# Local attention of a four-layer kernel: the next input's transposes in front of the second tile's scores, and their copy in front of the queries' squares

## The chip, the cores and the metric

The kernel runs on one core of one Trainium2 chip. Its time is the device time of one execution in microseconds; the median of three runs counts. A core has five engines with an instruction stream each: TensorE (PE, with its weight loads shown apart as PEld), VectorE (DVE), ScalarE (ACT), GpSimd (POOL) and SyncE (SP, which issues the DMAs). They run side by side and meet only at semaphores. Each engine works through its own stream in the order in which it is written.

## The reference

Four layers follow each other on an input of 32 sequences x 256 tokens x 128 features. The change touches the second, which runs twice (two local-attention blocks, each with a gated MLP behind it). Cut to what matters:

```python
x = x + layernorm(L0_attn(layernorm(x)))
x = x + layernorm(L0_ffn(layernorm(x)))       # two blocks of the kind below
x = x + layernorm(L1_attn(layernorm(x)))
x = x + layernorm(L1_ffn(layernorm(x)))

def _layer(x, ...):                           # 8 heads of 64, window 64
    h = shift_token(x)                        # half of the features from the token before
    q, k, v = split(h @ wqkv)
    q = l2norm(q) * qs; k = l2norm(k) * ksc
    q, k = rotary_xpos(q, k)
    o = local_attention(q, k, v)              # softmax over the own and the preceding window
    x = x + o @ wo
    ...                                       # gated MLP
```

## The kernel before

The function `window_attention` is built twice, as `w0` and `w1` (the page calls both `w`). A sequence of 256 tokens is one unit of work, two tiles of 128 tokens. A software pipeline of four stages runs over the 32 sequences: in step s, `ahead` is sequence s (its input is transposed), `front` is s-1 (keys, values and queries are projected, squared and turned), `back` is s-2 (scores, softmax, first tile's output) and `done` is s-3 (second tile's output, output projection). So 35 steps a layer; steps 0 to 3 and the last three are written out, those between are a loop of two steps a turn. In 29 steps of each layer (3 to 31) all four sequences exist.

The order on each engine is written by hand in its `step` function. The parts around the change:

- **TensorE** (`step`, L1428): keys of front, transposes KT, yT0, first half of the values V0, transposes QT, transposes P1 of done, masks and scores of tile 0 (job S0), attended values Y1 of done, V1, queries Q (L1376), transposes yT1 of done, masks and scores of tile 1 (S1, L1351 and L1364), the two transposes zT of ahead's input (L1392), transposes P0, the output projection "out" of done (L1469), attended values Y0 of back (L1414).
- **ScalarE** (`step`, L1310): squares and copy of the keys, copies kT, qT, pT of P1, yT0, V0, the exponentials of tile 0 (eight, L1305), copies of V1 and yT1 (L1269), squares of the queries (L1278), the two copies of zT into `hT` (L1334 for the features that stay, L1335 for those that are shifted by a token), copy of the queries (rawQ, L1269), the exponentials of tile 1.
- **VectorE** (`step`, L1205): among other work the maxima of tile 1's scores (L1180), the bias made from them (L1186, a 128x8 product), the copy of P0 out of PSUM (L1238), the lengths of the queries, and after Y0 its division (L1195).
- **GpSimd** (`step`, L1087): the rotary products of the keys and of the queries (two instructions each, L1071) and the powers of their lengths (L1084).

PSUM results go through rings of banks. The ring `short` has two banks and, in this order, six jobs a step: yT0, V0, V1, yT1, zT, out. Before TensorE writes a job (`wait_free`, L123) it waits until the job that had the same bank, two jobs earlier, has been copied out ("drained"). So V1 and zT share a bank, as do yT1 and out. "out" waits besides until zT has been copied (L1465), and so do the next sequence's keys (L1373). `hT` has one buffer: V1 and Q read it, then the copies of zT overwrite it.

Of the kernel before, what the change touches and what calls it, by code (L numbers as in the profile page):

```python
# [17 lines left out]
TILES = T // P  # L18
# [956 lines left out]
def window_attention(nc, n_seq, x, z, w, c, layer, shift, entry, following, leaving_stage):  # L975
# [14 lines left out]
    with ExitStack() as ctx:  # L990
# [49 lines left out]
        z_copy, copied = entry.z_copy, entry.copied  # L1040
# [13 lines left out]
        with nc.Block() as block:  # L1054
# [205 lines left out]
            @block.scalar  # L1260
            def _(act):
                act.wait_ge(setup, 6)
                c["ffn_loaded"].wait(act)

                def taken(job, seq, out, scatter=None):

                    of[job].wait_filled(act, job, seq)
                    source = of[job].bank(job, seq)[:, :]
                    nc.scalar.copy(out, scatter(source) if scatter else source)\  # L1269
                        .then_inc(of[job].drained.sem, 1)  # L1270

                def squared_(kind, front):
                    of[kind].wait_filled(act, kind, front)
                    if not front.first:

                        act.wait_ge(turn.sem, turn.done("cos." + kind, front.before()))
                        act.wait_ge(gps.sem, gps.done("sin1." + kind, front.before()))
                    nc.scalar.square(squares[kind][:, :, :].rearrange("p t e -> p (t e)"),  # L1278
                                     of[kind].bank(kind, front)[:, :]).then_inc(squared.sem, 1)

                def raw_taken(kind, front):
                    taken(kind, front, raw[kind][:, :, :].rearrange("p t e -> p (t e)"))

                def values_taken(t, front):
                    if t == 0 and not (isinstance(front.number, int) and front.number < 2):

                        act.wait_ge(moved[front.parity], moves(front) - 32)
                    taken(f"V{t}", front, v[front.parity][:, t, :, 0:HD],
                          lambda b: b.rearrange("p (h d) -> p h d", h=NH))

                def y_taken(t, done):
                    taken(f"yT{t}", done, yT[:, :, t * P:(t + 1) * P],
                          lambda b: b.rearrange("p (a q) -> p a q", a=PAIRS))

                def exps(t, back):
                    job, kept = f"S{t}", {0: "P0", 1: "P1"}[t]
                    scores = sided(of[job].bank(job, back), P)
                    if not back.first:

                        of[kept].wait_filled(act, kept, back.before())  # L1300
                    act.wait_ge(biased.sem, biased.done(str(t), back))
                    for side in range(SIDES):
                        for i in range(PAIRS):
                            h = t * NH + 2 * i + side
                            ins = nc.scalar.activation(  # L1305
                                probs[:, t, side, i, :], scores[:, side, i, :], ACT.Exp,
                                bias=bias[:, t, side, i:i + 1], scale=inv["Q"][back.parity][:, h:h + 1])
                    ins.then_inc(of[job].drained.sem, 1)

                def step(ahead, front, back, done):  # L1310
                    if front:
                        squared_("K", front)
                        raw_taken("K", front)
                    if back:
                        for job, out in (("KT", kT), ("QT", qT)):
                            taken(job, back, out[:, :, :].rearrange("p a (t j) -> p t a j", t=TILES),
                                  lambda b: b.rearrange("p (t a j) -> p t a j", t=TILES, a=PAIRS))
                    if done:
                        taken("P1", done, pT[:, 1].rearrange("p s i q -> p (s i q)"))
                        y_taken(0, done)  # L1320
                    if front:
                        values_taken(0, front)
                    if back:
                        exps(0, back)
                    if front:
                        values_taken(1, front)
                    if done:
                        y_taken(1, done)
                    if front:
                        squared_("Q", front)  # L1330
                    if ahead:
                        short.wait_filled(act, "zT", ahead)
                        bank = short.bank("zT", ahead)
                        nc.scalar.copy(hT[0:HD, :], bank[0:HD, 0:T])  # L1334
                        nc.scalar.copy(hT[HD:P, 1:T], bank[HD:P, 0:T - 1]).then_inc(short.drained.sem, 1)  # L1335
                    if front:
                        raw_taken("Q", front)
                    if back:
                        exps(1, back)

                pipeline(act, n_seq, step, 4)

            @block.tensor
            def _(pe):
# [42 lines left out]
                def transposed(job, seq, blocks):  # L1387

                    of[job].wait_free(pe, job, seq)
                    out = of[job].bank(job, seq)  # L1390
                    for b, block_ in enumerate(blocks):
                        ins = nc.tensor.transpose(out[:, b * P:(b + 1) * P], block_, c["ident"][:, :])  # L1392
                    ins.then_inc(of[job].filled.sem, 1)
# [30 lines left out]
                def y_transposed(t, done):  # L1424
                    of[f"Y{t}"].wait_drained(pe, f"Y{t}", done)
                    transposed(f"yT{t}", done, columns(y[:, t, :]))

                def step(ahead, front, back, done):  # L1428
                    if front:
                        projected("K", front)  # L1430
                    if back:
                        pe.wait_ge(turn.sem, turn.done("unit.K", back))
                        transposed("KT", back, [b for t in range(TILES) for b in columns(turned["K"][:, t, :])])
                    if done:
                        y_transposed(0, done)
                    if front:
                        values_projected(0, front)
                    if back:
                        pe.wait_ge(turn.sem, turn.done("add.Q", back))
                        transposed("QT", back, [b for t in range(TILES) for b in columns(turned["Q"][:, t, :])])  # L1440
                    if done:
                        probs_transposed(1, done)
                    if back:
                        masked(0, back)
                        ring_b.wait_drained(pe, "QT", back)
                        scores(0, back)
                    if done:
                        attended(1, done)
                    if front:
                        values_projected(1, front)  # L1450
                        projected("Q", front)
                    if done:
                        y_transposed(1, done)
                    if back:
                        masked(1, back)
                        scores(1, back)
                    if ahead:
                        pe.wait_ge(copied.sem, copied.done("z", ahead))
                        transposed("zT", ahead, [z_copy[:, t] for t in range(TILES)])
                    if back:  # L1460
                        probs_transposed(0, back)
                    if done:
                        short.wait_free(pe, "out", done)
                        if ahead:
                            short.wait_drained(pe, "zT", ahead)  # L1465
                        short.wait_drained(pe, "yT1", done)
                        for t in range(TILES):
                            for pair in range(PAIRS):
                                ins = nc.tensor.matmul(short.bank("out", done)[:, t * D:(t + 1) * D],  # L1469
                                                       yT[:, pair, t * P:(t + 1) * P],  # L1470
                                                       w["wo"][:, layer, pair, :],
                                                       start=pair == 0, stop=pair == PAIRS - 1)
                        ins.then_inc(short.filled.sem, 1)
                    if back:
                        attended(0, back)
# [1104 lines left out]
```

## Time and profile before

| | |
|---|---|
| median of 3 runs | 3916.48 us (3916.41 to 5067.23) |
| profiled execution: time, span | 3917.67 us, 3915.9 us |
| PE busy | 3738.0 us (95%) |
| DVE busy | 3055.1 us (78%) |
| ACT busy | 2629.5 us (67%) |
| POOL busy | 1953.2 us (50%) |
| mean granted TensorE clock | 0.986 |
| local attention w0 / w1 in the span | about 804 to 1424 us / 1566 to 2177 us |

The three runs are spread by one that took 5067.23 us; the other two agree within 0.1 us with each other and within 1.3 us with the profiled execution. The page sums each engine over the whole span; the two local-attention stages are a third of it, and only they are touched.

### The profile page before, as it was taken

Reading aid. Unit: us, or ns where it says so; the run is one execution under the profiler, and the core shown is the slowest. Engines: PE = TensorE matmul, PEld = TensorE weight load, DVE = VectorE, ACT = ScalarE, POOL = GpSimd, SP = SyncE. Lnnn points to the kernel's source line nnn. Section 1 sums busy time; section 2 is a strip of 40 time slices with the busy share of each in tenths; the row PEclk is TensorE's granted clock in tenths of the full one; section 3 lists DMA queues with packets and bytes.
Section 4 is the critical chain, followed back from the end, with each engine's and each line's share of the span. In section 5 each row is a group of like instructions: output and inputs, shape, how many; then the busy total and the mean of one; then the engine's idle time right before and its main releaser. Section 6 shows DMA issues by size and latency. Waiting matters only on the chain. (4 is left out here: it accounts for less than half of the span.)

```text
span 3915.9 us, 103685 instructions
## 1 busy us (share of the span) xinstructions
PE 3738.0 (95%) x34267; PEld 2885.6 (74%) x34457; DVE 3055.1 (78%) x7366; ACT 2629.5 (67%) x6409; POOL 1953.2 (50%) x1930
## 2 busy tenths in 40 slices
PE   7999999989999999999999999999999999999999
PEld 5777677657777766677777557777777777789998
DVE  6999999978888855888888677777777777766666
ACT  7999999858888843788888336666666666633333
POOL 4666666667777721667766334434434444411111
PEclk9999999989999989999999899999999999999999
DMA  3000000000000011000000110000000000000000
GB/s 109 1 0 0 0 0 0 1 19 21 22 23 20 20 26 25 15 16 14 14 16 19 25 36 2 0 0 0 0 0 0 0 0 0 1 8 8 9 9 9
DMA packets 69051, 47.63 MB, mean 12 GB/s; under 512 B 38360, under 2 KB 57952, under 8 KB 68832
## 3 DMA queue, kind: packets, MB, share of 16 engines
q1 hardware_dynamic: 68960, 46.43, 4.7%
q8 instruction: 55, 0.90, 0.1%
q14 instruction: 36, 0.29, 0.0%
HBM read 12.62 MB, written 4.19 MB: 4 GB/s over the span
## 5 line engine op out<-in xcount | busy, mean ns | idle before, releaser
L1896 ACT ACTIVATE l_probs<-l_act,l_neg_max 128x128 f32<-128x128 f32 (+1 forms) x1024 | 415.9, 425 | 382.9 <-DVE l_neg_max L1830 382.8
L1803 POOL TENSOR_TENSOR l_probs<-l_probs,l_sums 128x512 f32<-128x512 f32 x384 | 393.0, 1041 | 437.7 <-DVE l_sums L1848 437.7
L613 POOL TENSOR_TENSOR t_probs<-t_probs,t_neg_max 128x512 f32<-128x512 f32 x384 | 391.5, 1041 | 245.8 <-DVE t_neg_max L682 245.7
L2224 ACT ACTIVATE e_hT<-e_act 128x512 f32<-128x512 f32 x256 | 152.8, 597 | 286.9 <-PE e_act L2245 286.9
L672 DVE SCALAR_TENSOR_TENSOR t_probs<-t_tanh_qk,scalars_sb,t_dve 128x512 f32<-128x512 f32 x384 | 269.3, 742 | 72.1 <-ACT t_tanh_qk L787 41.9
L1824 DVE TENSOR_TENSOR l_act<-l_act,mask_rows 128x256 f32<-128x256 f32 (+1 forms) x384 | 178.5, 510 | 146.8 <-PE l_act L1951 146.8
L1084 POOL TENSOR_TENSOR w_invQ<-w_lengthsQ,minus_half 128x16 f32<-128x16 f32 x64 | 244.0, 3812 | 87.4 <-DVE w_lengthsQ L1157 87.4
L2257 PEld LDWEIGHTS e_dve<-e_sb,e_hT 128*128 128x128 f32 x2048 | 269.7, 192 | 15.7 <-ACT e_hT L2224 2.6
L1071 POOL TENSOR_TENSOR w_swappedQ<-w_rawQ,w_table 128x512 f32<-128x512 f32 x128 | 162.2, 1290 | 236.6 <-ACT w_rawQ L1269 236.6
L2257 PE MATMUL e_dve<-e_sb,e_hT 128*128 128x128 f32 x2048 | 270.8, 275 | 1.8 <-ACT e_hT L2224 1.8
L2245 PE MATMUL e_act<-e_xnT,e_sb 128*128 128x256 f32 x1024 | 267.3, 384 | 0.0
L787 ACT ACTIVATE t_tanh_qk<-t_act,t_inv_beta 128x512 f32<-128x512 f32 x384 | 245.2, 699 | 28.3 <-PE t_act L848 28.2
L1376 PE MATMUL w_c<-wqkv_sb,w_hT 128*128 128x512 f32 x512 | 255.1, 622 | 6.1 <-ACT w_rawQ L1269 3.7
L1839 DVE COPY l_pT<-l_dve 128x512 f32<-128x512 f32 x384 | 244.9, 678 | 1.0 <-PE l_dve L1962 1.0
L848 PE MATMUL t_act<-t_k,t_q 32*128 32x256 f32 (+1 forms) x2048 | 220.4, 343 | 25.8 <-DVE t_probs L672 25.0
L1830 DVE TENSOR_REDUCE l_neg_max<-l_act 128x2 f32<-128x512 f32 (+1 forms) x384 | 245.0, 678 | 0.0
L682 DVE TENSOR_REDUCE t_neg_max<-t_probs 128x2 f32<-128x512 f32 (+1 forms) x384 | 243.4, 674 | 0.0
L1305 ACT ACTIVATE w_probs<-w_a,w_bias,w_invQ 128x128 f32<-128x128 f32 x512 | 186.0, 469 | 82.8 <-DVE w_bias L1186 82.8
L804 ACT ACTIVATE t_probs<-t_probs 128x512 f32<-128x512 f32 x384 | 230.6, 656 | 13.3 <-POOL t_probs L613 13.1
L1071 POOL TENSOR_TENSOR w_swappedK<-w_rawK,w_table 128x512 f32<-128x512 f32 x128 | 223.7, 1769 | 7.2 <-ACT w_rawK L1269 7.2
L1951 PE MATMUL l_act<-l_kT,l_qT 64*128 64x128 f32 (+1 forms) x2048 | 219.6, 343 | 3.2 <-ACT l_probs L1896 3.0
L854 PE MATMUL t_dve<-t_bits,t_left 32*128 32x256 f32 (+1 forms) x2048 | 220.5, 343 | 0.0
(256 smaller groups left out, 10400.8 us busy)
## 6 DMA issues: line engine op xcount, KB each, us to landing
w_v_mid<-w_v SPq DMA_DIRECT2D x128, 130.0 KB, 2.3
z<-w_z_copy SPq DMA_DIRECT2D x32, 128.0 KB, 2.0
h<-z SPq DMA_DIRECT2D x32, 128.0 KB
out<-x_sb SPq DMA_DIRECT2D x32, 128.0 KB, 1.8
h<-z SPq DMA_DIRECT2D x32, 127.0 KB
wqkv_sb<-L_ffn_wqkv SPq DMA_DIRECT2D x2, 768.0 KB, 6.7
kv_up_sb<-L_attn_w_kv_up SPq DMA_DIRECT2D x1, 1024.0 KB, 9.3
e_sb<-L_ffn_w SPq DMA_DIRECT2D x1, 1024.0 KB, 5.6
```

What stands on the lines that cost most here:

```text
L613: nc.gpsimd.tensor_tensor(p, p, neg_max[:, j, 0:len(gs)].unsqueeze(2) .broadcast_to((P, len(gs), P * (t + 1))), ALU.add).then_inc(shifted. ...
L672: nc.vector.scalar_tensor_tensor(probs[:, j % SLOTS, :], tanh_qk[:, j % TANHS, :], alpha, to_dve.bank("bil" + name, back)[:, :], ALU.mult, ...
L787: nc.scalar.activation(tanh_qk[:, j % TANHS, :], to_act.bank("raw" + name, back)[:, :], ACT.Tanh, scale=inv_beta[:, :])\
L1071: nc.gpsimd.tensor_tensor(swapped[kind][:, t, :].rearrange("p (h a d) -> p h a d", a=2, d=HD // 2), raw[kind][:, t, :].rearrange("p (h a d ...
L1084: nc.gpsimd.tensor_tensor(inv[kind][seq.parity][:, :], length[kind][:, :], c["minus_half"][:, 0:TILES * NH], ALU.pow).then_inc(gps.sem, 1)
L1376: ins = nc.tensor.matmul(of[kind].bank(kind, front)[:, t * BANK:(t + 1) * BANK], hT[:, t * P:(t + 1) * P], w["wqkv"][:, layer, at:at + INNER],
L1803: nc.gpsimd.tensor_tensor(p, p, sums[:, at, 0:len(hs)].unsqueeze(2) .broadcast_to((P, len(hs), P * (t + 1))), ALU.mult).then_inc(divided.s ...
L1830: nc.vector.tensor_reduce(neg_max[:, units.index(name), 0:len(hs)], to_act.bank("s" + name, back)[:, :].rearrange("p (h j) -> p h j", h=le ...
L1839: nc.vector.tensor_copy(pT[:, units.index(name), :], to_dve.bank(job, seq)[:, :])\
L1896: ins = nc.scalar.activation(probs[:, at % SLOTS, s * width:(s + 1) * width], bank[:, s * width:(s + 1) * width], ACT.Exp, bias=neg_max[:, ...
L2245: ins = nc.tensor.matmul(to_act.bank(f"h{e}", back)[:, f * T:(f + 1) * T], w["e1"][:, e, f * P:(f + 1) * P], xnT[back.parity][:, :], start ...
L2257: ins = nc.tensor.matmul(to_dve.bank(job, seq)[:, (e % half) * D:(e % half + 1) * D], hT[:, e % 2, f, t * P:(t + 1) * P], w["e2"][:, e, f, :],
```

## The change

In the TensorE `step` the two transposes zT (with their wait for the input) move from behind tile 1's scores to in front of tile 1's masks and scores. In the ScalarE `step` the two copies of zT move from behind the squares of the queries to in front of them. No instruction is added or removed; VectorE's, GpSimd's and SyncE's streams are the same, and so is the order of the ring's jobs.

```diff
@@ -1326,13 +1326,13 @@
                     if done:
                         y_taken(1, done)
-                    if front:
-                        squared_("Q", front)
                     if ahead:
                         short.wait_filled(act, "zT", ahead)
                         bank = short.bank("zT", ahead)
                         nc.scalar.copy(hT[0:HD, :], bank[0:HD, 0:T])
                         nc.scalar.copy(hT[HD:P, 1:T], bank[HD:P, 0:T - 1]).then_inc(short.drained.sem, 1)
+                    if front:
+                        squared_("Q", front)
                     if front:
                         raw_taken("Q", front)
@@ -1451,12 +1451,12 @@
                     if done:
                         y_transposed(1, done)
+                    if ahead:
+                        pe.wait_ge(copied.sem, copied.done("z", ahead))
+                        transposed("zT", ahead, [z_copy[:, t] for t in range(TILES)])
                     if back:
                         masked(1, back)
                         scores(1, back)
-                    if ahead:
-                        pe.wait_ge(copied.sem, copied.done("z", ahead))
-                        transposed("zT", ahead, [z_copy[:, t] for t in range(TILES)])
                     if back:
                         probs_transposed(0, back)
```

TensorE, step 3 of the first layer, before; short0 and short1 are the ring's two banks, a step of the loop has the same sequence:

```order
L1383 MATMUL w0_short1<-wqkv_sb,w0_hT 128x512 [waits w0_short_drained]
L1376 MATMUL w0_c<-wqkv_sb,w0_hT 128x512 [waits w0_c_drained]
L1376 MATMUL w0_c<-wqkv_sb,w0_hT 128x512
L1392 MATMUL w0_short0<-ident_sb,w0_y 128x128 [waits w0_short_drained,w0_b_drained]
L1392 MATMUL w0_short0<-ident_sb,w0_y 128x128 x3
L1351 MATMUL w0_b<-w0_masks,ident_bf 128x512 [waits w0_b_drained]
L1351 MATMUL w0_b<-w0_masks,ident_bf 128x512
L1364 MATMUL w0_b<-w0_kT,w0_qT 64x128 x16
L1392 MATMUL w0_short1<-ident_sb,w0_z_copy 128x128 [waits w0_short_drained,w0_copied]
L1392 MATMUL w0_short1<-ident_sb,w0_z_copy 128x128
```

The same place in the changed kernel:

```order
L1383 MATMUL w0_short1<-wqkv_sb,w0_hT 128x512 [waits w0_short_drained]
L1376 MATMUL w0_c<-wqkv_sb,w0_hT 128x512 [waits w0_c_drained]
L1376 MATMUL w0_c<-wqkv_sb,w0_hT 128x512
L1392 MATMUL w0_short0<-ident_sb,w0_y 128x128 [waits w0_short_drained,w0_b_drained]
L1392 MATMUL w0_short0<-ident_sb,w0_y 128x128 x3
L1392 MATMUL w0_short1<-ident_sb,w0_z_copy 128x128 [waits w0_short_drained,w0_copied]
L1392 MATMUL w0_short1<-ident_sb,w0_z_copy 128x128
L1351 MATMUL w0_b<-w0_masks,ident_bf 128x512 [waits w0_b_drained]
L1351 MATMUL w0_b<-w0_masks,ident_bf 128x512
L1364 MATMUL w0_b<-w0_kT,w0_qT 64x128 x16
```

The transposes of z_copy, with their wait for the ring, now stand ahead of the masks and scores that go to bank pair b. They write bank short1, which V1 (the first row) has filled.

ScalarE, the same step, before:

```order
L1305 ACTIVATE w0_probs<-w0_a,w0_bias,w0_invQ1 128x128 x7
L1269 COPY w0_v0<-w0_short1 128x8x64 [waits w0_short_filled]
L1269 COPY w0_yT<-w0_short0 128x4x128 [waits w0_short_filled]
L1278 ACTIVATE w0_squaresQ<-w0_c 128x1024 [waits w0_gps,w0_turn,w0_c_filled]
L1334 COPY w0_hT<-w0_short1 64x256 [waits w0_short_filled]
L1335 COPY w0_hT<-w0_short1 64x255
L1269 COPY w0_rawQ<-w0_c 128x1024 [waits w0_c_filled]
```

And in the changed kernel:

```order
L1305 ACTIVATE w0_probs<-w0_a,w0_bias,w0_invQ1 128x128 x7
L1269 COPY w0_v0<-w0_short1 128x8x64 [waits w0_short_filled]
L1269 COPY w0_yT<-w0_short0 128x4x128 [waits w0_short_filled]
L1332 COPY w0_hT<-w0_short1 64x256 [waits w0_short_filled]
L1333 COPY w0_hT<-w0_short1 64x255
L1278 ACTIVATE w0_squaresQ<-w0_c 128x1024 [waits w0_gps,w0_turn,w0_c_filled]
L1269 COPY w0_rawQ<-w0_c 128x1024 [waits w0_c_filled]
```

The two hT copies changed places with the squares; the copy of V1 out of short1 (second row) stays behind tile 0's exponentials.

## Rows read from the trace of the kernel before

**Rows 1.** Windows of one step, w0: span, PE busy (count), clock, DMA, GB/s
```profile
1007.50:1026.00 18.50, 17.89 (x170) 1.00 0.09 21
```
**Rows 2.** Waits, stretch 804 to 1424: engine, line, waited for: total us, times, longest
```profile
PE w_short L1469 <- ACT w_hT L1335: 14.1, 28, 0.5
```
**Rows 3.** Timeline of PE, w0: start us, duration us, line, out<-in, count [idle]
```profile
1006.03 1.90 PE L1414 MATMUL w_a<-w_v,w_pT 128*128 128x65 f32 x16
...
1018.83 0.60 PE L1392 MATMUL w_short<-ident_sb,w_y 128*128 128x128 f32 x4
1019.48 0.38 PE L1351 MATMUL w_b<-w_masks,ident_bf 128*128 128x512 bf16 x1
1019.79 1.10 PE L1364 MATMUL w_b<-w_kT,w_qT 64*64 64x128 f32 x32
1020.83 0.44 PE L1392 MATMUL w_short<-ident_sb,w_z_copy 128*128 128x128 f32 x2
1021.10 1.04 PE L1392 MATMUL w_a<-ident_sb,w_probs 128*128 128x128 f32 x8
1022.65 2.05 PE L1469 MATMUL w_short<-wo_sb,w_yT 128*128 128x128 f32 x16 [0.51 <-ACT w_hT L1335]
1024.54 1.90 PE L1414 MATMUL w_a<-w_v,w_pT 128*128 128x65 f32 x16
```
**Rows 4.** Timeline of ACT, the same step of w0
```profile
1019.97 0.62 ACT L1269 COPY w_v<-w_short 128x512 f32<-128x512 f32 x1
...
1020.91 1.09 ACT L1278 ACTIVATE w_squaresQ<-w_c 128x1024 f32<-128x1024 f32 x1
1021.83 0.39 ACT L1334 COPY w_hT<-w_short 64x256 f32<-64x256 f32 x1
1022.23 0.37 ACT L1335 COPY w_hT<-w_short 64x255 f32<-64x255 f32 x1
1022.62 1.01 ACT L1269 COPY w_rawQ<-w_c 128x1024 f32<-128x1024 f32 x1
```
**Rows 5.** Timeline of PE, w1
```profile
1817.12 1.90 PE L1414 MATMUL w_a<-w_v,w_pT 128*128 128x65 f32 x16
...
1830.88 1.10 PE L1364 MATMUL w_b<-w_kT,w_qT 64*64 64x128 f32 x32
...
1835.13 1.90 PE L1414 MATMUL w_a<-w_v,w_pT 128*128 128x65 f32 x16
```
**Rows 6.** Timeline of ACT, w1: the copy of V1
```profile
1830.56 0.63 ACT L1269 COPY w_v<-w_short 128x512 f32<-128x512 f32 x1
```
**Rows 7.** Timeline of DVE, w1: maxima of tile 1, bias, copy of P0
```profile
1832.06 1.22 DVE L1180 TENSOR_REDUCE w_top<-w_b 128x8 f32<-128x1024 f32 x1 [0.37 <-PE w_b L1364]
1833.31 0.17 DVE L1186 TENSOR_TENSOR w_bias<-w_top,w_invQ 128x8 f32<-128x8 f32 x1
1833.41 1.23 DVE L1238 COPY w_pT<-w_a 128x1024 f32<-128x1024 f32 x1
```
**Rows 8.** Timeline of POOL, w0: the rotary products of the queries
```profile
1023.71 2.50 POOL L1071 TENSOR_TENSOR w_swappedQ<-w_rawQ,w_table 128x512 f32<-128x512 f32 x2 [3.70 <-ACT w_rawQ L1269]
```
**Rows 9.** Timeline, DVE beside POOL: two near-simultaneous starts, w1 and w0
```profile
1823.92 1.23 DVE L1165 TENSOR_TENSOR w_turnedK<-w_rawK,w_table 128x1024 f32<-128x1024 f32 x1
1823.93 3.63 POOL L1071 TENSOR_TENSOR w_swappedK<-w_rawK,w_table 128x512 f32<-128x512 f32 x2
...
845.67 1.28 DVE L1157 TENSOR_TENSOR w_lengthsK<-w_lengthsK,w_tiny 128x16 f32<-128x16 f32 x1
845.65 3.57 POOL L1071 TENSOR_TENSOR w_swappedK<-w_rawK,w_table 128x512 f32<-128x512 f32 x2
```
**Rows 10.** Timeline of PE, w0: keys of step 2
```profile
817.91 3.78 PE L1376 MATMUL w_c<-wqkv_sb,w_hT 128*128 128x512 f32 x4 [1.87 <-ACT w_rawQ L1269]
```
**Rows 11.** Timeline of PE, w0, step 2: attended values behind an idle stretch
```profile
836.52 3.27 PE L1414 MATMUL w_a<-w_v,w_pT 128*128 128x65 f32 x16 [2.70 <-DVE w_pT L1238]
```
**Rows 12.** Windows of PE behind that idle stretch (columns as in Rows 1)
```profile
840.00:843.50 3.50, 3.50 (x6) 0.50 0.02 5
```

## Prediction

> **What bounds the kernel now.** I read the windows of the two local-attention stages first, one window a step. In w0 TensorE is busy 17.89 of 18.50 us at a granted clock of 1.00 [rows 1]: it is the engine that sets the step. Next the waits: its only regular wait is that of the output projection "out" for the copy of hT, 14.1 us in 28 waits, 0.5 each [rows 2]. Then the timelines of one step. The step of w0 lasts 1024.54 - 1006.03 = 18.51 us [rows 3], that of w1 1835.13 - 1817.12 = 18.01 us [rows 5]; w1 has next to no such wait. In the w0 step the reader sees P0's transposes end at 1021.10 + 1.04 = 1022.14, and "out" start at 1022.65, behind 0.51 of idle time that ends with the hT copy (1022.23 + 0.37 = 1022.60, so 0.05 from ScalarE's end to TensorE's start) [rows 3, 4]. That wait is what an earlier zT can remove: with the copies in front of the squares of the queries hT would be ready 0.92 us earlier (squares 1020.91, next 1021.83).
>
> **The change part by part.** Nothing is added or removed, so all cost lies in waits.
>
> The ScalarE part by itself costs nothing in a loop step: copies (0.79 from 1021.83 to 1022.62) and squares (0.92) swap, and the copy of the queries behind both starts as before. The squares are late by 0.79, which VectorE's lengths of the queries hide: they are taken only after the bias and the P0 copy.
>
> The TensorE part is another matter. zT shares its bank with V1, and V1 is copied by ScalarE behind tile 0's exponentials: in w0 at 1019.97, done at 1020.59 [rows 4]. In the kernel before zT started at 1020.83, 0.24 later, with the scores of tile 1 in between as cover. Now it is wanted right behind yT1's transposes, which start at 1018.83 and are through when the masks start behind them, at 1019.48 at the latest [rows 3]. So TensorE stands still from about 1019.43 to 1020.59 + 0.05 = 1020.64, 1.2 us, and its queue behind it (masks and scores of tile 1, P0, out, Y0, and the next step's keys) stands too. The wait for the hT copy (0.51) is replaced by a longer one in front.
>
> Does ScalarE get to V1 earlier in the new rhythm? No: V1's copy hangs on TensorE through a chain that the change leaves alone. Call E the end of the attended values Y0 (L1414): behind it come VectorE's division, the keys and queries, tile 0's scores, their maxima and bias, and the exponentials. In w0 E is 1006.03 + 1.90 = 1007.93 and V1 is copied at 1020.59: 12.66 later, so zT can start at z = E + 12.71 [rows 3, 4]. In w1 E = 1819.02 and V1's copy ends at 1830.56 + 0.63 = 1831.19: z = E + 12.22 [rows 5, 6].
>
> From z to the next E, by rows 3: zT itself and the step to the masks 0.49 (two transposes 0.44, and the 0.05 that lie between yT1's end 1019.43 and the masks); masks to scores 0.31; scores to the next transposes 1.04; P0's eight transposes to "out" 0.95 (no row shows this step without the wait: at most their duration of 1.04; at least 0.88, since eight take 1.04 and yT1's four 0.60, 0.11 for one more; I take a value between); out to Y0 1.89; Y0 1.90. Sum 6.58. The first term is unknown too: zT to P0 was only 0.27, and that is its lower bound. So E to E is 12.71 + 6.58 = 19.29 in w0 (18.51 before, +0.78) and 12.22 + 6.58 = 18.80 in w1 (18.01 before, +0.79).
>
> Can the others follow? Tile 1's maxima start 1.18 behind the start of its scores (1830.88, 1832.06), the bias 1.25 behind them and the P0 copy 0.10 behind that, 1.23 long [rows 5, 7]. From z that is 0.49 + 0.31 + 1.18 + 1.25 + 0.10 + 1.23 = 4.56, plus 0.05; Y0 is due at z + 4.68. It fits with 0.07 to spare, so VectorE is nearly the bound too, and an overrun would show as a wait of L1414.
>
> Steps: 29 in each layer have done, back and ahead, so 29 x (0.78 + 0.79) = 45.5 us. In step 2 zT does not wait (fewer jobs in the ring), in the last three there is no zT. In step 1 the squares now stand behind a zT that waits for its input, so the copy of the queries is 0.92 later and with it the next keys, which wait for it [rows 4, 10]: 0.9 a layer, 1.8. Sum +47.3: the profiled execution's 3917.67 becomes 3965, its span 3915.9 becomes 3963; the median lies 1.2 below the profiled time, so 3964.
>
> Bounds of the unknown terms: z to masks 0.27 instead of 0.49 and P0 to out 0.88 give 0.29 less a step, 58 steps, -17: 3947. P0 to out at 1.04 gives +5, and VectorE's overrun up to 0.1 a step +6: 3975.
>
> **The rivals.** *GpSimd takes the port before the bias.* In the new rhythm two starts nearly coincide. The bias of tile 1 (a product of two SBUF operands) starts at z + 0.49 + 0.31 + 1.18 + 1.25 = z + 3.23. The rotary product of the queries starts 0.08 behind the end of their copy (1023.63, 1023.71) [rows 4, 8]: from z that is 0.48 to the first hT copy, 0.79, 0.92, 1.01, 0.08 = z + 3.28. What happens then two pairs of rows show [rows 9]. Where VectorE started at 1823.92 and GpSimd at 1823.93, VectorE's product took its 1.23 and GpSimd's pair took 3.63 instead of the 2.50 of rows 8. Where GpSimd started first, at 845.65, VectorE's 128x16 instruction of 845.67 took 1.28, where the 128x8 bias takes 0.17. So the first wins, by 0.01 or 0.02. Here VectorE leads by 0.05 on sums that are good to some 0.05, so it is likely, not sure, to win. If it loses, the bias is done 1.28 behind z + 3.28, at 4.56 instead of 3.40: the P0 copy and Y0 are late by about 1.04 (1.16 less spare and rounding), 29 x 1.04 = 30 us a layer. One layer: 3994; both: 4024, slower by 2.7%. It decides once GpSimd starts ahead of z + 3.23.
> The Trainium skill, "SBUF — State Buffer", section on the two separate sides, states this as an exclusive lock, held for a whole instruction by whichever starts first, with two SBUF inputs on VectorE against a GpSimd instruction that reads SBUF; by that rule the bias would wait for one of GpSimd's two instructions, and rows 9 agree with their 1.28.
>
> *The gain arrives, the bank is free.* If V1 were drained before yT1 is through, zT would start at once and "out" would lose its wait: 0.51 in 29 steps of w0 and at most 0.1 in those of w1, -15 - 3, + 1.8: 3901, faster than before by 0.4%. It decides at the copy of V1 ending before 1019.43 where the row says 1020.59; only a ring that does not bind as I read it would do it.
>
> *The clock.* Behind an idle stretch of 2.70 us in step 2 the attended values took 3.27 instead of 1.90 us [rows 3, 11], and the granted clock was 0.50 afterwards (the 1.2 GHz level) [rows 12]. If the new stop of 1.2 us brought that in every step, it would cost 1.37 and half of 3.50, 3.1 us a step, +180 in 58 steps: 4144. Against it: the wait of 0.51 leaves the clock at 1.00 in every step [rows 1], the new one is less than half of 2.70, and dense work stands on both sides.
>
> *A smaller stop.* Part of the chain from E to V1 has slack that I don't see, and half of the 47 us appears: 3940.
>
> **How the numbers follow.** The forecast, +47 us or 1.2%, gets 0.62. GpSimd first: 0.18 (0.12 in both layers, 0.06 in one). Smaller stop 0.11, gain 0.03, clock 0.04, something else slower 0.02. The forecast's own range is 3945 to 3976. For 8 in 10 the GpSimd rival has to be in it: 3945 to 4028. About 2% (78 us, so above 3995 or below 3838) is what a measurement of this kernel can tell from no change: slower has 0.12 + 0.04 + 0.02 = 0.18, faster 0.01, within 2% the other 0.81.
>
> **What would show it.** Right: in the timeline zT starts 0.05 behind the end of V1's copy with some 1.2 us of idle TensorE in w0 and 0.8 in w1 in front of it; the wait list names w_v for L1392 and no longer w_hT for L1469; steps of 19.3 and 18.8 us; V1's copy still 12.66 and 12.17 behind E. The GpSimd rival: L1186 of tile 1 at 1.2 instead of 0.17, and a new wait of L1414 for w_pT. The clock: windows under 1.00 in the loop. Wrong from the ground up: zT starts ahead of the end of V1's copy, or steps stay at 18.5 and 18.0.

## The result, and the profile after

| | before | after |
|---|---|---|
| median | 3917.23 us (4 runs, 3916.41 to 5067.23) | 3956.57 us (4 runs, 3954.24 to 3958.99) |
| ratio, 95% interval | | 1.0105 [1.0092, 1.0117] |
| profiled execution: time, span | 3917.67, 3915.9 us | 3958.99, 3957.2 us |
| mean granted TensorE clock | 0.986 | 0.991 |
| a step of w0 / w1 in the loop | 18.50 / 18.01 us | 19.37 / 18.88 us |

The change costs 39.3 us on the medians and 41.3 us between the two profiled executions. 47.3 was forecast. One of before's four runs took 5067.23 us; without it the median is 3916.48 and the cost 40.1 us, and the ratios, here and below, leave such a run out. They are worked out from all the other runs and differ from the ratios of the medians by about 0.001. The page's busy times hardly move; TensorE and VectorE do the same work in a longer span:

```profile
PE 3736.1 (94%) x34267; PEld 2877.1 (73%) x34457; DVE 3054.7 (77%) x7366; ACT 2640.1 (67%) x6409; POOL 1950.5 (49%) x1930
```

The waits of w0 after the change (stretch 804 to 1450; engine, line, waited for: total us, times, longest us):

```profile
DVE w_top L1180 <- PE w_b L1364: 42.2, 31, 2.2
PE w_short L1392 <- ACT w_v L1269: 34.4, 29, 1.2
```

and of w1 (1590 to 2200):

```profile
PE w_short L1392 <- ACT w_v L1269: 21.0, 29, 1.1
```

The wait of L1469 for the copy of hT [rows 2] has no line any more. In its place the transposes zT wait for the copy of V1, 29 times a layer: 34.4 / 29 = 1.19 us each in w0, 0.72 in w1. VectorE's maxima of tile 1 (L1180) wait for the scores behind that stop.

TensorE in one step of w0 (start us, duration us, line, out<-in, count, idle before it); it answers to [rows 3]:

```profile
1047.15 0.60 PE L1392 MATMUL w_short<-ident_sb,w_y 128*128 128x128 f32 x4
1048.93 0.44 PE L1392 MATMUL w_short<-ident_sb,w_z_copy 128*128 128x128 f32 x2 [1.19 <-ACT w_v L1269]
1049.43 0.38 PE L1351 MATMUL w_b<-w_masks,ident_bf 128*128 128x512 bf16 x1
1050.77 1.09 PE L1392 MATMUL w_a<-ident_sb,w_probs 128*128 128x128 f32 x8
1051.70 1.95 PE L1469 MATMUL w_short<-wo_sb,w_yT 128*128 128x128 f32 x16
1053.63 1.97 PE L1414 MATMUL w_a<-w_v,w_pT 128*128 128x65 f32 x16
```

ScalarE in the same step; it answers to [rows 4]:

```profile
1048.26 0.62 ACT L1269 COPY w_v<-w_short 128x512 f32<-128x512 f32 x1
1049.41 0.36 ACT L1332 COPY w_hT<-w_short 64x256 f32<-64x256 f32 x1
1050.18 1.02 ACT L1278 ACTIVATE w_squaresQ<-w_c 128x1024 f32<-128x1024 f32 x1
1051.10 1.01 ACT L1269 COPY w_rawQ<-w_c 128x1024 f32<-128x1024 f32 x1
```

VectorE and GpSimd in the same step:

```profile
1052.16 0.17 DVE L1186 TENSOR_TENSOR w_bias<-w_top,w_invQ 128x8 f32<-128x8 f32 x1
1052.18 2.52 POOL L1071 TENSOR_TENSOR w_swappedQ<-w_rawQ,w_table 128x512 f32<-128x512 f32 x2 [3.87 <-ACT w_rawQ L1269]
1052.26 1.22 DVE L1238 COPY w_pT<-w_a 128x1024 f32<-128x1024 f32 x1
```

The reader sees yT1's transposes end at 1047.75, V1's copy end at 1048.88 and zT start at 1048.93, 0.05 behind it, with 1.19 of idle TensorE in front; "out" follows P0's transposes without a gap; and the bias of tile 1 starts 0.02 ahead of GpSimd's rotary product and takes its normal 0.17. This lead is 0.02 in every loop step of both layers.

### The profile page after: what moved, and what is told of

It is laid out like the page before. It is cut to its first block and busy times, and to the rows that moved or that the text cites. A ratio compares the mean times of both kernels' runs of the same rounds, so it can differ in the third digit from the quotient of the medians.

```text
span 3957.2 us, 103685 instructions
## 1 busy us (share of the span) xinstructions
PE 3736.1 (94%) x34267; PEld 2877.1 (73%) x34457; DVE 3054.7 (77%) x7366; ACT 2640.1 (67%) x6409; POOL 1950.5 (49%) x1930
```

## The experiments

All edits are made to the kernel before or to the changed one, as each says. The times of before beside them are medians of 7 runs: 3919.41 us for the first four, 3909.5 us for the others.

### The TensorE half alone

Kernel before with zT moved in front of tile 1's scores; ScalarE keeps the squares in front of the hT copies.

```diff
+                    if ahead:
+                        pe.wait_ge(copied.sem, copied.done("z", ahead))
+                        transposed("zT", ahead, [z_copy[:, t] for t in range(TILES)])
                     if back:
                         masked(1, back)
                         scores(1, back)
-                    if ahead:
-                        pe.wait_ge(copied.sem, copied.done("z", ahead))
-                        transposed("zT", ahead, [z_copy[:, t] for t in range(TILES)])
```

> Only the TensorE half of the change: zT in front of tile 1's scores, ScalarE's order as before (squares of the queries, then the copies of zT). Theory (stop for V1's bank, and a coincidence of two starts): the stop is the same, so without more the step is that of the changed kernel, 19.37 us in w0 and 18.89 in w1, and the time 3955. But now ScalarE does not wait for zT: its squares start behind yT1's copy at about z + 0.27, the copy of the queries ends at z + 2.98, and GpSimd's rotary product starts at z + 3.06, ahead of the bias of tile 1 at z + 3.23. So the bias should take about 1.1 instead of 0.17 us, and the attended values Y0 come 0.9 to 1.0 later: 58 x 0.95 = +55, about 4008. Rival (the two do not disturb each other here, or the bias is not on the path): L1186 stays at 0.17 us and the time at 3955.

Measured: 4016.35 us, ratio 1.0255 [1.0237, 1.0274], steps of 20.30 (w0) and 19.82 us (w1). The steps are those forecast for GpSimd going first (19.37 + 0.95); the median lies 8 us above the 4008 expected, the profiled execution, 4012.12, 4 above. Timeline of w0, ScalarE, GpSimd, VectorE and TensorE:

```profile
1116.60 0.44 PE L1392 MATMUL w_short<-ident_sb,w_z_copy 128*128 128x128 f32 x2 [1.20 <-ACT w_v L1269]
1116.87 1.09 ACT L1278 ACTIVATE w_squaresQ<-w_c 128x1024 f32<-128x1024 f32 x1
1118.57 1.01 ACT L1269 COPY w_rawQ<-w_c 128x1024 f32<-128x1024 f32 x1
1119.66 2.49 POOL L1071 TENSOR_TENSOR w_swappedQ<-w_rawQ,w_table 128x512 f32<-128x512 f32 x2 [3.69 <-ACT w_rawQ L1269]
1119.83 1.12 DVE L1186 TENSOR_TENSOR w_bias<-w_top,w_invQ 128x8 f32<-128x8 f32 x1
1122.23 1.97 PE L1414 MATMUL w_a<-w_v,w_pT 128*128 128x65 f32 x16 [0.92 <-DVE w_pT L1238]
```

The stop at zT is the same 1.20. But ScalarE squares while TensorE makes zT, so the copy of the queries starts 1.97 behind zT instead of the 2.17 of the changed kernel (1051.10 - 1048.93), and GpSimd starts 3.06 behind zT instead of 3.25. The bias starts at 3.23 in both. GpSimd is first by 0.17, the bias takes 1.12 instead of 0.17, the copy of P0 behind it is late, and the attended values Y0 wait 0.92: 20.30 - 19.37 = 0.93 a step. So the half that I called free is what keeps the changed kernel from a further 53 us of span (4010.3 against 3957.2).

### The ScalarE half alone

Kernel before with the hT copies moved in front of the squares of the queries, TensorE as it was.

```diff
-                    if front:
-                        squared_("Q", front)
                     if ahead:
                         short.wait_filled(act, "zT", ahead)
                         ...
+                    if front:
+                        squared_("Q", front)
```

> Only the ScalarE half: the copies of zT in front of the squares of the queries, TensorE's order as before. Theory: no stop for V1, since tile 1's scores cover it; ScalarE waits 0.4 us for zT, hT is ready 0.5 earlier and the output projection's wait of 0.51 in w0 goes; squares and copy of the queries come 0.4 later, which nobody waits for. w0 steps 18.0, w1 steps 17.9: -15 - 3 + 2 = 3901. Rival (the ScalarE half is what costs, because the queries are late): above 3930.

Measured: 3887.62 us, ratio 0.9927 [0.9906, 0.9948], steps of 17.96 in both layers. Timeline of w0, ScalarE and TensorE:

```profile
1126.66 0.37 ACT L1332 COPY w_hT<-w_short 64x256 f32<-64x256 f32 x1 [0.22 <-PE w_short L1392]
1127.46 2.05 PE L1469 MATMUL w_short<-wo_sb,w_yT 128*128 128x128 f32 x16
```

"out" starts without idle time and the 0.51 of [rows 3] are gone: 18.50 - 17.96 = 0.54 a step. The step is now as long as TensorE's own work in [rows 1], 17.89, but for 0.07. The change therefore holds a gain and a larger loss, and the loss is all in TensorE's half. The two halves don't add: alone they give -28 and +94 us of span, together +41. Two things overlap. With TensorE's half alone "out" doesn't wait for hT either, so the gain of 0.54 a step of w0 is in both halves and counts once; and the ScalarE half decides who is first in the pair above, which takes 0.93 off. In w0 that is -0.54 + 1.80 + 0.54 - 0.93 = 0.87 a step, as measured. (The median stands lower than the 3901 expected; the steps came as expected, and the rest lies outside them, see the passages below.)

### The wait without the move

Kernel before, with no instruction moved, and one wait more on TensorE: tile 1's masks wait until V1 has been copied.

```diff
                     if done:
                         y_transposed(1, done)
+                    if done and ahead:
+                        short.wait_drained(pe, "V1", front)
                     if back:
                         masked(1, back)
                         scores(1, back)
```

> The kernel before with one wait more on TensorE: in the 29 full steps it waits in front of tile 1's masks until V1 has been copied out of its bank; no instruction moves. Theory: this wait is the whole loss. Masks then start with V1's copy done, 12.7 (w0) and 12.2 us (w1) behind the end of Y0, and the step grows by 0.7 to 0.87 us in both layers: 3957 to 3967. Rival (the loss comes from the new order, such as zT in front of the scores or the late queries, and a wait here is absorbed): below 3930.

Measured: 3964.47 us, ratio 1.0124 [1.0106, 1.0142], steps of 19.34 and 18.85 us, which are the changed kernel's to 0.03. TensorE in w0, with the last copy of hT and VectorE's copy of P0:

```profile
1125.40 0.38 PE L1351 MATMUL w_b<-w_masks,ident_bf 128*128 128x512 bf16 x1 [1.43 <-ACT w_v L1269]
1127.02 1.04 PE L1392 MATMUL w_a<-ident_sb,w_probs 128*128 128x128 f32 x8
1127.59 0.37 ACT L1335 COPY w_hT<-w_short 64x255 f32<-64x255 f32 x1
1128.01 2.05 PE L1471 MATMUL w_short<-wo_sb,w_yT 128*128 128x128 f32 x16
1128.23 1.22 DVE L1238 COPY w_pT<-w_a 128x1024 f32<-128x1024 f32 x1
1129.90 1.90 PE L1414 MATMUL w_a<-w_v,w_pT 128*128 128x65 f32 x16
```

The stop is 0.24 longer than the changed kernel's 1.19, and zT's transposes now come behind the scores; the two even out. "out" has no idle time in front of it here either: hT is ready at 1127.96, and P0's transposes end at 1128.06. So in this kernel too the new stop takes the place of the old wait. Nothing has to be transposed early to lose this time; it is enough that TensorE's queue stands behind the copy of V1.

### The bank drained early

Changed kernel, with ScalarE's copy of V1 taken in front of tile 0's exponentials instead of behind them.

```diff
-                    if back:
-                        exps(0, back)
                     if front:
                         values_taken(1, front)
+                    if back:
+                        exps(0, back)
                     if done:
                         y_taken(1, done)
```

> The changed kernel, with ScalarE's copy of V1 moved from behind to in front of tile 0's exponentials; the ring's order is kept. Theory: zT's bank is free when zT is wanted, the stop goes, and the exponentials come 0.5 to 1.1 us later, inside the slack in front of P0's transposes. Steps 18.0 in w0 and 17.9 in w1: 3896 to 3905, faster than the kernel before. Rival (the bank is not what zT waits for, or the exponentials have no slack): 3940 or more.

Measured: 3890.12 us, ratio 0.9928 [0.9907, 0.9949], steps of 17.95 us in both layers. As with the ScalarE half alone the steps came as expected and the median is lower (3896 to 3905 was expected). Timeline of w0:

```profile
1120.99 0.59 ACT L1269 COPY w_v<-w_short 128x512 f32<-128x512 f32 x1 [1.63 <-PE w_short L1383]
1122.51 0.60 PE L1392 MATMUL w_short<-ident_sb,w_y 128*128 128x128 f32 x4
1122.94 0.38 PE L1392 MATMUL w_short<-ident_sb,w_z_copy 128*128 128x128 f32 x2
1123.38 0.38 PE L1351 MATMUL w_b<-w_masks,ident_bf 128*128 128x512 bf16 x1
```

V1 is out of the bank 1.36 before zT wants it, and the stop is gone. Together with the kernel above, which makes the stop by the wait alone, this shows the wait for the copy of V1 to be the whole of the loss. The early zT itself brings nothing over the ScalarE half (3890.12 against 3887.62): with the wait of "out" gone either way, the step is TensorE's work.

### Who is first: 0.16 us in front of the bias, or behind it

Two kernels that differ in the place of one instruction. Both are the changed kernel with a copy of one PSUM column (128x1) added to VectorE in tile 1; it is in nobody's way by itself. First in front of the bias:

```diff
                     after(f"max.{t}", back)
+                    if t:
+                        nc.vector.tensor_copy(c["carrier"][:, 2:3], of[job].bank(job, back)[:, 0:1])
                     nc.vector.tensor_tensor(
                         bias[:, t], top[:, t],
```

> The changed kernel with one copy of a single column (128x1, from PSUM) on VectorE between tile 1's maxima and its bias, in both layers; its result is not used. Theory (whoever starts first holds the shared port): in the changed kernel the bias starts 0.02 us ahead of GpSimd's rotary product of the queries; about 0.1 us later it starts behind it, takes about 1.2 instead of 0.17 us, and Y0 comes about 1.0 later in each of 58 steps: about 4016. Rival (the two share the port without blocking each other, and the 1.12 us of the TensorE-only kernel has another cause): the copy costs its own 0.1 us a step, 3962.

then behind the bias, in front of the copy of P0:

```diff
                         ring_a.wait_filled(dve, "P0", back)
+                        nc.vector.tensor_copy(c["carrier"][:, 2:3], ring_a.bank("P0", back)[:, 0:1])
                         nc.vector.tensor_copy(pT[:, 0].rearrange("p s i q -> p (s i q)"),
```

> The same 128x1 copy from PSUM, but behind the bias and in front of the copy of P0, in both layers. Theory: the bias keeps its lead of 0.02 us over GpSimd and takes 0.17; the copy of P0, which sets the start of Y0, comes 0.1 later: 58 x 0.1 = +6, about 3962. Rival (any 0.1 us on VectorE costs a microsecond here): about 4016.

Measured: 4045.4 us, ratio 1.0353 [1.0332, 1.0374] in front, and 3962.29 us, ratio 1.0147 [1.0122, 1.0172] behind. The same 0.16 us of work costs 83 us more at the one place than at the other. In front, w0:

```profile
1121.20 0.44 PE L1394 MATMUL w_short<-ident_sb,w_z_copy 128*128 128x128 f32 x2 [1.21 <-ACT w_v L1271]
1124.43 0.16 DVE L1187 COPY carrier<-w_b 128x1 f32<-128x1 f32 x1
1124.44 2.49 POOL L1071 TENSOR_TENSOR w_swappedQ<-w_rawQ,w_table 128x512 f32<-128x512 f32 x2 [3.88 <-ACT w_rawQ L1271]
1124.51 1.23 DVE L1188 TENSOR_TENSOR w_bias<-w_top,w_invQ 128x8 f32<-128x8 f32 x1
1127.01 1.97 PE L1416 MATMUL w_a<-w_v,w_pT 128*128 128x65 f32 x16 [1.10 <-DVE w_pT L1240]
```

Behind, w0:

```profile
1128.74 0.17 DVE L1186 TENSOR_TENSOR w_bias<-w_top,w_invQ 128x8 f32<-128x8 f32 x1
1128.76 2.52 POOL L1071 TENSOR_TENSOR w_swappedQ<-w_rawQ,w_table 128x512 f32<-128x512 f32 x2 [3.88 <-ACT w_rawQ L1270]
1128.84 0.16 DVE L1238 COPY carrier<-w_a 128x1 f32<-128x1 f32 x1
1128.91 1.22 DVE L1239 COPY w_pT<-w_a 128x1024 f32<-128x1024 f32 x1
```

In front, the bias starts 0.07 behind GpSimd and ends at 1125.74, which is when the first of GpSimd's two instructions ends (1124.44 + 2.49 / 2 = 1125.69), and Y0 waits 1.10; the step goes from 19.37 to 20.49. Behind, GpSimd's start is the same 0.02 after the bias, and the step grows by 0.08 (19.45 and 18.96): the copy of P0 starts 0.17 behind the bias instead of 0.10 (1052.16, 1052.26). The same reckoning holds for the kernel with the copy in front: its bias starts 3.31 behind zT (1124.51 - 1121.20) instead of 3.23, 0.08 later, and is held for 1.23 - 0.17 = 1.06; together 1.14, and the step grew by 1.12. The copies out of PSUM (L1187, L1238, L1239) keep their duration beside GpSimd; the product of two SBUF operands does not. The Trainium skill, "SBUF — State Buffer", section on the two separate sides, says the same: an exclusive lock, taken by the first to start, between a VectorE instruction with two SBUF inputs and a GpSimd instruction that reads SBUF.

The kernel with the copy in front was expected at 4016 and came at 4045. The profiled execution took 4036.49, the least of the four runs (up to 4050.52), so 20 us of the surplus can be looked up. 7 of them are the price itself: 1.12 a step where 1.0 was expected, 58 times. The rest has a cause that was not in the theory. In w1 half of the steps are 20.00 us, but seven are 21.5 to 21.7, each followed by one of 20.3 (the last by 20.1). One of the seven, TensorE, and the windows over it (span, PE busy with count, granted clock, DMA share, GB/s):

```profile
1727.28 0.44 PE L1394 MATMUL w_short<-ident_sb,w_z_copy 128*128 128x128 f32 x2 [0.71 <-ACT w_v L1271]
1733.10 2.08 PE L1416 MATMUL w_a<-w_v,w_pT 128*128 128x65 f32 x16 [1.10 <-DVE w_pT L1240]
1734.97 3.56 PE L1378 MATMUL w_c<-wqkv_sb,w_hT 128*128 128x512 f32 x4
...
1756.88 1.94 PE L1378 MATMUL w_c<-wqkv_sb,w_hT 128*128 128x512 f32 x4
```

```profile
1732.00:1734.00 2.00, 0.91 (x8) 1.00 0.00 0
1734.00:1736.00 2.00, 2.00 (x12) 0.70 0.00 0
1736.00:1738.00 2.00, 2.00 (x4) 0.50 0.00 0
1738.00:1740.00 2.00, 2.00 (x14) 0.94 0.00 0
```

The stop of 1.10 ends at 1733.10; some 1.7 us later, with TensorE at work, the granted clock falls to 0.50, the 1.2 GHz level, and the keys take 3.56 instead of the 1.94 of the next step. The seven pairs cost about 7 x (1.67 + 0.30) = 13.8 us. What the other three runs have above this one no trace shows. The Trainium skill, "TensorE: Matmul & The Clock Gate", section on a second failure mode, tells of a clock that swings because TensorE idles briefly between groups of matmuls, and these windows agree in so far as no longer stop lies in front of the fall. Why it takes these seven steps, and none of w0, where the stops are 1.21 and 1.10, no run here shows; and TensorE's half alone, with stops of 1.20 and 0.92, keeps its clock in every loop step.

### The kernel before, twice more

No edit: how far does one kernel move by itself, outside its loop steps?

> The kernel before, unchanged, for a second trace. Theory (part of the difference to the changed kernel lies outside the steps and is not the change's): the steps are again 18.50 and 18.01 us to 0.01, while the passage from w0 to the gated MLP and its end, from w0's last kT copy to w1's first, which took 186.2 us before and 179.8 after, takes between 178 and 187 us and goes with the granted clock of those stretches. Rival (the passage is a property of the kernel): 186.2 us again, within 0.5.

> The kernel before, unchanged, a third trace, for the same reason and with the same expectations: steps of 18.50 and 18.01 us; the passage from w0's last kT copy to w1's first between 178 and 187 us with the granted clock, against 186.2 us within 0.5 for the rival.

Measured: 3913.44 and 3909.02 us. The loop steps are 18.50 / 18.01 and 18.48 / 18.00, as in the first profile. The passage from w0's last copy of kT to w1's first, in which the change touches next to nothing, took 179.0 and 184.5 us here, 186.2 in the first profile of before, 179.8 in the changed kernel, and 178.6 to 185.6 in the six others. It goes with the granted clock: the mean over the passage is 0.91 where it took 186.2, 0.94 where it took 185.6 and 184.5, 0.96 at 182.9, and 0.97 or 0.98 in the six traces of 178.6 to 180.9. The windows behind the end of w0, of before:

```profile
1416.80:1422.80 6.00, 3.57 (x38) 3.03 (x39) 1.48 (x5) 1.62 (x3) 0.00 (x0) 0.50 0.01 3
1422.80:1428.80 6.00, 4.39 (x20) 3.73 (x19) 1.70 (x11) 0.71 (x1) 0.53 (x1) 0.50 0.09 19
```

and of after (span; PE, PEld, DVE, ACT, POOL busy with counts; granted clock, DMA share, GB/s):

```profile
1442.30:1448.30 6.00, 3.69 (x52) 3.16 (x50) 2.26 (x7) 0.83 (x2) 0.00 (x0) 1.00 0.01 3
1448.30:1454.30 6.00, 4.79 (x14) 2.32 (x15) 3.49 (x17) 3.43 (x4) 1.74 (x3) 1.00 0.15 32
```

The kernel before had 1.2 GHz at this place in its first profile, and the changed one 2.4. The 14 runs of the kernel before beside the experiments lie from 3901.65 to 3919.59 us, 18 us apart, though its loop steps keep to 0.02.

## Why the prediction was right, step by step

**The mechanism: shown.** zT starts 0.05 behind the end of V1's copy, with 1.19 (w0) and 0.72 us (w1) of idle TensorE before it (forecast 1.2 and 0.8). The wait alone makes the whole loss, and draining the bank early removes it.

**The fixed chain from E to V1: right.** In the step shown E is 1036.24 (the attended values of the step before, 1034.27 + 1.97) and V1's copy ends at 1048.88: 12.64, where 12.66 was used. Why w1's chain is shorter by 0.49 the prediction left open. The trace names a likely cause, the bias of tile 0. In w0, after the change:

```profile
1042.09 3.36 POOL L1071 TENSOR_TENSOR w_swappedK<-w_rawK,w_table 128x512 f32<-128x512 f32 x2
1044.76 0.71 DVE L1186 TENSOR_TENSOR w_bias<-w_top,w_invQ 128x8 f32<-128x8 f32 x1
```

This bias is held as the one of tile 1 was in the experiments: it takes 0.71 and ends 0.02 behind GpSimd's product of the keys. In w1 it starts behind that product and takes 0.17. Before the change it is the same, with 0.72. So both kernels seem to pay about 0.54 us (an estimate, 0.71 - 0.17) a step of w0 for such a coincidence, ahead of tile 0's exponentials and so of V1's copy. No run takes it away, so this is not shown.

**The sum from z to the next E: 6.67, not 6.58.** From the TensorE rows after: zT to masks 0.50 (0.49 used), P0 to "out" 0.93 (0.95), "out" to Y0 1.93 (1.89), Y0 itself 1.97 (1.90); masks to P0 is 1.34 (1.35). The terms that fell short are the last two, and the likely cause is the engine named as having 0.07 to spare: VectorE. Its copy of P0 ends at 1053.48, and the weight loads of Y0 start 0.12 behind it:

```profile
1053.60 1.86 PEld L1414 LDWEIGHTS w_a<-w_v,w_pT 128*128 128x128 f32 x16
```

The trace shows no wait of L1414 for this, which was to be my sign; but in the kernel with a copy behind the bias P0's copy is 0.07 later and the step 0.08 longer, so no slack is left between VectorE and Y0. The kernel with the wait alone supports this: there P0's copy ends 0.45 ahead of Y0 (1129.45, 1129.90), "out" to Y0 is 1.89 and Y0 takes 1.90, the values that were forecast. With 6.67 the step is 12.64 + 0.05 + 6.67 = 19.36, measured 19.37. The overrun of 0.1 a step stood among the bounds (+6 us).

**The steps: +0.87 each where +0.78 and +0.79 were forecast.** Over the 29 steps of each layer it is 25.1 + 25.2 = 50.3 us against 45.5.

**Outside the steps: -9 us, where +1.8 was forecast.** The first and last intervals between copies of kT are 0.9 and 0.9 shorter in w0, 0.5 and 0.7 in w1; the passage is 6.3 shorter, the rest behind w1 1.9 shorter, the start 2.2 longer: 50.3 - 3.0 - 6.3 - 1.9 + 2.2 = 41.3, as measured. All that lies outside these 58 intervals takes 2856.8, 2852.8 and 2848.5 us in the three traces of before and 2847.7 after. With no edit it moves by 8.3, so nearly all of these 9 us can come without any edit; counted by the steps, the change costs 50 us. The later keys of the ramp were there: 2.78 of wait in step 2 against 1.87 [rows 10], 0.9 a layer, but they drown in this. The forecast of 3964 lies 7 us above the 3957 measured because the steps cost 5 more than forecast and the parts outside them came out 11 lower, which no view of the kernel before alone could tell. That the sum came so near is in part luck; the 0.87 a step against 0.78 is the fairer measure.

**GpSimd before the bias: did not happen, by 0.02.** The lead was put at 0.05 "on sums that are good to some 0.05"; it is 0.02 in both layers. A lead inside the error of its own sum is luck as much as reckoning, and the forecast's 47 us hung on it. The price was about right: the TensorE half alone, where GpSimd leads, is 0.93 a step above the changed kernel, and the kernel with the copy in front 1.12, for which 1.04 was put.

**The ScalarE half "costs nothing": right in the sum, but too small a role.** I weighed it by its cover alone. It holds a gain of 0.54 a step by itself, which I named only as a rival for the whole change, and it is what puts GpSimd behind the bias.

**The clock.** The clock stays at 1.00 throughout the changed kernel's loops, as forecast. My reason, that 1.2 us is less than half of 2.70 and dense work stands on both sides, was weaker than I took it for: in the kernel with the copy in front, with two stops in a step, 0.71 and 1.10, seven steps of w1 did lose the clock. 0.04 was thin for it.

**What would have been the better change.** Two edits keep the gain without the stop: the ScalarE half alone (ratio 0.9927) or the whole change with V1 copied first (0.9928). Both bring the step to 17.96 or 17.95, within 0.1 of TensorE's own work; hardly any time is left there for a change of order.

## What to carry to other kernels

Before a producer is moved forward in a ring of PSUM banks, look up who used its bank last and when that user's copy ends: moved ahead of that point it stops the whole queue behind it, and the cover that made the old wait free is exactly the work it was moved past. Test the two halves of an edit that touches two engines one by one; here one half was worth -0.7% and the other +2.6%. Where a product of two SBUF operands on VectorE and a GpSimd instruction start close to each other (here 0.02 to 0.17 us), work out the order of the two starts for every edit, on either engine or on those that feed them: here a lead of 0.02 us kept away a loss of 0.9 to 1.1 us a step.

## What the runs showed of the hardware

VectorE's 128x8 product took 0.17 us when it started 0.02 ahead of GpSimd, and 1.12 and 1.23 us when it started 0.17 and 0.07 behind: in each case to 0.02 us behind the end of the first of GpSimd's two instructions, not of both. So the engines do not meet only at semaphores, as the opening section has it; these two also meet here. A 128x1 copy from PSUM that started 0.01 ahead of GpSimd did not keep GpSimd waiting (2.49 for its pair) and lost nothing itself.

The granted clock fell to the 1.2 GHz level inside a loop of otherwise dense work with stops of 0.71 and 1.10 us a step, in seven of the steps of one layer; with stops of 1.21 and 1.10 in the other layer, and in a loop with one stop of 1.2 us a step, it did not. And between stages one and the same kernel was at 1.2 GHz in one execution and at 2.4 in another, at the same place, and the 14 executions of the kernel before beside the experiments are spread over 18 us, 0.5%: one execution of each of two kernels can't tell less than that, but their steps can.
